# A step count of the dense work ahead of each token-row scatter on POOL

## The chip, the cores and the metric

One Trainium2 chip, of which the kernel uses one core. The metric is the device time of one execution in microseconds, as the median of the runs. The engines are TensorE (PE), VectorE (DVE), ScalarE (ACT), GpSimd (POOL) and SyncE (SP), which here only issues transfers.

## What is computed

A block of attention and a mixture of experts over x of shape (2, 1024, 128), that is 2048 token rows of 128 channels:

```python
x = x + layernorm(attention(layernorm(x)))
x = x + layernorm(ffn(layernorm(x)))

def ffn(x):                              # 64 experts of width 88, 8 of them per token
    scores = sigmoid(x @ gate_w.T)
    choice = scores + gate_bias
    # the best 4 of 8 groups by the sum of their top two, then the best 8 experts in them
    w = scores[chosen] / sum(scores[chosen]) * 2.5
    routed = sum over chosen e of w[e] * (silu(x @ Wg[e].T) * (x @ Wu[e].T)) @ Wd[e].T
    return routed + (silu(x @ Sg.T) * (x @ Su.T)) @ Sd.T
```

## The kernel before

The 2048 tokens are four quads of 512 (16 tiles of 128). After the attention and the routing, the experts are computed in two ways. Quads 2 and 3 (`DENSE`) go through all 64 experts. Quads 0 and 1 (`SPARSE`, eight tiles, `ST = 8`) are sorted by expert: each token row is written eight times, once for each chosen expert, into an array `pair_x` in HBM at a slot that the routing gave; this is the scatter. Later a pair stage, the "burst", reads `pair_x` back in tiles of 128 rows of one expert each, applies that expert and writes `pair_y`, from which eight gathers a tile bring the results back.

**Dense steps.** A step is one of the gate, up and down products of 16 experts' 8 hidden channels for one quad. On TensorE it is six products for gate and up (`gate_up`, L1765 to L1767) and, two steps later (`LAG = 2`), a down product (`down`, L1794, recorded as two matmuls). ScalarE applies SiLU (L1004), VectorE multiplies by the route weight (L1308) and then the two halves (L1318); this last instruction raises the semaphore `s_hid` by one. Steps 0 to 7 are the shared expert (L1507 on VectorE), steps 8 to 15 the first routed ones, and from step 16 on come rounds of eight steps; the burst stands after round 4, so after step 47. When step n has been through VectorE, `s_hid` is n + 1.

**Scatters.** POOL issues 64 scatters (`scatter`, L743): for tile t of the eight and chosen expert k of the eight, an indirect DMA of 128 rows of 512 bytes. `POOL_ORDER` (written out by hand) puts scatters I0 and I1, which are k = 0 to 3 of tile 0, between the last operations of the routing, and I2 to I31 behind all of them. Before the first scatter of a tile POOL waits until all eight of the tile before have landed:

```python
if half == 0:
    pool.wait_ge(s_slots, t + 1)
    if t >= 1:
        pool.wait_ge(s_scat[t - 1], 16 * CHOSEN)
```

Behind the scatters POOL has nothing but the gathers, which wait for the burst's last results (L754).

**What waits for the scatters.** Only SyncE. It issues transfers in a fixed order: dense weights into `w_raw` (`reload`, L630, which waits for the down product that frees the buffer), after each of them three pieces of the weights of the burst (`gu_w`, `down_w`, L614), and, ahead of the dense weights number 27:

```python
if n == BEFORE - 1:
    load_late(len(late))
    for t in range(ST):
        sp.wait_ge(s_scat[t], 16 * CHOSEN)
    for g in range(4):
        load_pairs(g)
```

`load_pairs` (L620) reads four tiles of `pair_x`. Just ahead of it stands `reload(26)`, which waits for the down product of step 45. On TensorE the burst begins with `turn_pairs` (L1945), which waits for the first of these loads.

Of the kernel before, what the change touches and what calls it, by code (L numbers as in the profile page):

```python
# [54 lines left out]
def build(nc, x, w_basis_t, w_v, b_v, w_o_t, b_o, gate_w_t, gate_bias, w_experts, w_shared_up,  # L55
# [21 lines left out]
    CHOSEN = TOP_GROUPS * GE // 4  # L77
# [17 lines left out]
    with ExitStack() as ctx:  # L95
# [8 lines left out]
        def sem(name):  # L104
            return ctx.enter_context(nc.semaphore(name))
# [194 lines left out]
        s_hid = sem("hidden_ready")  # L300
# [151 lines left out]
        SHARED_STEPS = QUADS * SHARED  # L452
# [96 lines left out]
        SUM_AT = {at + 2: t for at, t in WEIGH_AT.items()}  # L549
        MOMENTS_AT = {at + 3: t for at, t in WEIGH_AT.items()}  # L550
        FINISH_AT = {at + 5: t for at, t in WEIGH_AT.items()}

        block = ctx.enter_context(nc.Block())

# [115 lines left out]
        def _(pool):  # L670
# [61 lines left out]
            def scatter(n):  # L732

                t, half = n // 4, n % 4
                if n == 0:
                    pool.wait_ge(s_fill, 16 * (PAIR_TILES // 8))
                    pool.wait_ge(s_xn2, len(SPARSE))
                if half == 0:
                    pool.wait_ge(s_slots, t + 1)
                    if t >= 1:  # L740
                        pool.wait_ge(s_scat[t - 1], 16 * CHOSEN)
                for k in (2 * half, 2 * half + 1):
                    g.indirect_dma_start(  # L743
                        pair_x, bass.IndirectOffsetOnAxis(ap=slots[:, t, k:k + 1], axis=0),
                        x2_rows[:, t, :], None).then_inc(s_scat[t], 16)
# [110 lines left out]
            for what, q, _ in POOL_ORDER:  # L856
                if what in "SX":
                    inv_sqrt(NORMS.index((what, q)), buffer_of(what, q), what == "X")
                elif what == "D":
                    inv_sqrt_att(q)  # L860
                elif what == "B":
                    make_select()
                elif what == "K":
                    make_rank_constants()
                elif what == "I":
                    scatter(q)
                elif what == "P":
                    norm_x(q)
                elif what == "M":
                    write_route(q)  # L870
                elif what == "F":
                    add_bias(q)
                elif what == "J":
                    mask_groups(q)
                elif what == "L":

                    pool.wait_ge(s_shhi, q + 1)
                    n = WD if q == 0 else GATE_AT + REST
                    g.tensor_tensor(sh_lo[:, q, 0:n], sh_raw[:, q, 0:n], sh_hi[:, q, 0:n],
                                    ALU.subtract).then_inc(s_shlo, 1)  # L880
                elif what == "R":
                    split_lo(q)
                elif what == "E":
                    low_part(q)
# [269 lines left out]
        def _(dve):  # L1154
# [275 lines left out]
            def moments(t):  # L1430

                own = t % 2
                if t == 0:
                    dve.wait_ge(s_ysht, len(SPARSE))
                dve.wait_ge(s_red, t + 1)
                link(tt(total[:, own, :], total[:, own, :], shared_y[:, t, :], ALU.add))
                link(v.bn_stats(f_stats[:, own, :], total[:, own, :]))
                v.bn_aggr(f_mv[:, own, :], f_stats[:, own, :]).then_inc(s_fvar, 1)

            def finish(t):  # L1440

                own = t % 2
                dve.wait_ge(s_frstd, t + 1)
                link(v.tensor_scalar(total[:, own, :], total[:, own, :], f_mv[:, own, 0:1],
                                     f_rstd[:, own:own + 1], ALU.subtract, ALU.mult))
                tt(x_sb[:, t, :], total[:, own, :], x1_sb[:, t, :], ALU.add).then_inc(s_fy, 1)
# [69 lines left out]
            for r, k in ROUND_STEPS:  # L1516
# [12 lines left out]
                if at in MOMENTS_AT:  # L1529
                    moments(MOMENTS_AT[at])  # L1530
                if at in FINISH_AT:
                    finish(FINISH_AT[at])

# [581 lines left out]
```

## Time and profile before

| | us |
|---|---|
| median of 3 runs | 421.49 |
| lowest and highest | 420.11 and 421.81 |
| span of the profiled execution | 451.5 |
| mean granted clock of TensorE in it | 0.952 |

The span runs from the first to the last instruction of the one execution that was profiled; a separate time of that execution is not given. It is 30.0 us longer than the median of the timed runs, so a sum of microseconds read from the profile has to say whether the stretch it stands on is there in the timed runs too. Times in the profile are counted from the span's start. The stages are, roughly: attention and routing to 100 us, with the first dense steps from some 75 us on; dense steps with the scatters beside them from 86 to 200 us; the burst to 304 us; dense steps with the gathers beside them, and the sparse tiles' last norms, to the end.

### The profile page before, as it was taken

What the parts mean: (1) busy time and instruction counts of PE and PEld (TensorE: products, weight loads), DVE (VectorE), ACT (ScalarE), POOL (GpSimd) and SP (SyncE); (2) the same over time, 40 slices, a digit from 0 to 9 for tenths busy, and PEclk for the clock granted to TensorE, in tenths of its full rate; (3) what the DMA queues carried; (4) which work ended last, traced back from release to release, by engine and by line L of the source; (5) the groups of instructions that cost most, each with busy time, mean ns of one, the idle gap of its engine ahead of it and who ended that gap; (6) DMA issues with size and microseconds to landing.
All of it is one profiled execution on the core that took longest, in us unless ns stands there. A gap on an engine that the chain in (4) does not pass through costs nothing.

```text
span 451.5 us, 7319 instructions
## 1 busy us (share of the span) xinstructions
PE 399.2 (88%) x2023; PEld 301.9 (67%) x2024; DVE 288.2 (64%) x761; ACT 212.9 (47%) x557; POOL 184.8 (41%) x242
## 2 busy tenths in 40 slices
PE   7889997789999969979999999999749979897784
PEld 5779775355665646646999999996526656564563
DVE  5756987854566635661666666546338867694884
ACT  3668884234234312322666666663144524453424
POOL 7574554666665456600000000004734747667001
PEclk9999996789999998996999999999969989999998
DMA  6369200011489866223666666542211313231001
GB/s 174 112 247 404 97 2 1 12 37 46 159 260 298 203 165 162 81 78 110 179 181 171 181 180 174 168 116 76 71 47 54 99 46 99 82 94 54 13 6 46
DMA packets 65467, 54.03 MB, mean 120 GB/s; under 512 B 7013, under 2 KB 61333, under 8 KB 65429
## 3 DMA queue, kind: packets, MB, share of 16 engines
q1 hardware_dynamic: 60469, 44.85, 33.3%
q0 software_dynamic: 4096, 8.40, 6.4%
q10 hardware_dynamic: 864, 0.33, 0.3%
q8 instruction: 18, 0.29, 0.3%
q14 instruction: 20, 0.16, 0.1%
HBM read 31.53 MB, written 22.02 MB: 119 GB/s over the span
## 4 chain that ended last, share of the span: by engine, by line
PE 67%; DVE 11%; another core or an unknown queue 7%; issue 5%; POOL 5%; ACT 3%; DMA 1%; POOLq 0%; DVEq 0%; SPq 0%; ACTq 0%
PE ps L1794 13%; PE ps L1967 9%; PE ps L1765 8%; PE ps L1767 8%; PE ps L1766 8%; PE ps L1992 6%; PE ps L1945 3%; PE ps L1979 3%; DVE up_w L1308 3%; DVE hid L1318 2%; PE ps L1717 2%; PE ps L1656 1%; PE ps L1705 1%; PE ps L1898 1%
## 5 line engine op out<-in xcount | busy, mean ns | idle before, releaser
L1765 PE MATMUL ps<-x_hi,w_hi 128*128 128x512 f32 (+1 forms) x184 | 98.3, 534 | 25.9 <-DVE hid L1318 24.4
L754 POOL DMA_INDIRECT picked<-pair_y,slots x64 | 62.9, 983 | 137.2 <-DMA pair_y<-pair_out 118.7
L1004 ACT ACTIVATE ps<-ps 128x512 f32<-128x512 f32 (+1 forms) x92 | 51.6, 564 | 137.0 <-PE ps L1767 78.5
L1308 DVE TENSOR_TENSOR up_w<-ps,route_w 128x512 f32<-128x512 f32 (+1 forms) x92 | 61.2, 665 | 73.4 <-remote 31.4
L1794 PE MATMUL ps<-hid,w_raw 128*128 128x512 f32 (+1 forms) x182 | 94.1, 600 | 0.6 <-DVE hid L1318 0.6
L743 POOL DMA_INDIRECT pair_x<-x_rows,slots x64 | 62.5, 977 | 39.5 <-issue 21.0
L1765 PEld LDWEIGHTS ps<-x_hi,w_hi 128*128 128x128 f32 x184 | 35.5, 193 | 62.8 <-issue 34.8
L1767 PE MATMUL ps<-x_hi,w_lo 128*128 128x512 f32 (+1 forms) x184 | 72.3, 393 | 0.0
L1766 PE MATMUL ps<-x_lo,w_hi 128*128 128x512 f32 (+1 forms) x184 | 71.9, 391 | 0.0
L1318 DVE TENSOR_TENSOR hid<-ps,up_w 128x512 f32<-128x512 f32 (+1 forms) x92 | 61.5, 668 | 6.0 <-issue 2.3
L1401 DVE COPY pair_ht<-ps 88x256 f32<-88x256 f32 x64 | 26.9, 421 | 37.4 <-PE ps L1979 30.8
L1967 PE MATMUL ps<-gu_w,pair_xt 128*128 x256 | 50.0, 318 | 0.0
L1766 PEld LDWEIGHTS ps<-x_lo,w_hi 128*128 128x128 f32 x184 | 35.4, 192 | 17.8 <-issue 13.5
L1794 PEld LDWEIGHTS ps<-hid,w_raw 128*128 128x128 f32 x182 | 35.3, 198 | 8.8 <-issue 1.0
L1767 PEld LDWEIGHTS ps<-x_hi,w_lo 128*128 128x128 f32 x184 | 35.4, 192 | 7.6
L1967 PEld LDWEIGHTS ps<-gu_w,pair_xt 128*128 128x128 f32 x256 | 38.9, 192 | 1.4 <-issue 1.0
L1992 PE MATMUL ps<-down_w,pair_ht 88*128 x256 | 39.2, 275 | 0.1
L1035 ACT COPY pair_out<-ps 128x256 f32<-128x256 f32 x64 | 23.9, 373 | 22.8 <-PE ps L1992 22.8
L1992 PEld LDWEIGHTS ps<-down_w,pair_ht 88*128 88x128 f32 x256 | 33.6, 191 | 0.3 <-issue 0.3
L1945 PE MATMUL ps<-ident,pair_in 128*128 128x128 f32 x128 | 25.3, 279 | 4.1 <-DMA pair_in<-pair_x 3.7
L1028 ACT ACTIVATE pair_g<-ps 128x176 f32<-128x176 f32 x64 | 20.3, 318 | 16.0 <-PE ps L1967 15.9
L1019 ACT COPY pair_xt<-ps 128x256 f32<-128x256 f32 x64 | 24.1, 377 | 6.2 <-PE ps L1945 6.2
(220 smaller groups left out, 586.1 us busy)
## 6 DMA issues: line engine op xcount, KB each, us to landing
w_raw<-in_w_experts SPq DMA_DIRECT2D x44, 192.0 KB
pair_x<-zero SPq DMA_DIRECT2D x16, 512.0 KB, 5.6
pair_in<-pair_x SPq DMA_DIRECT2D x32, 256.0 KB, 3.0
pair_y<-pair_out SPq DMA_DIRECT2D x64, 128.0 KB, 2.2
gu_w<-in_w_experts SPq DMA_DIRECT2D x22, 256.0 KB
down_w<-in_w_experts SPq DMA_DIRECT2D x16, 176.0 KB
pair_x<-x_rows,slots POOLq DMA_INDIRECT x64
picked<-pair_y,slots POOLq DMA_INDIRECT x64
```

Of the source, the lines that this page charges most:

```text
L743: g.indirect_dma_start(pair_x, bass.IndirectOffsetOnAxis(ap=slots[:, t, k:k + 1], axis=0), x2_rows[:, t, :], None).then_inc(s_scat[t], 16)
L754: g.indirect_dma_start(picked[:, t % 3, k, :], None, pair_y, bass.IndirectOffsetOnAxis(ap=slots[:, t, k:k + 1], axis=0)).then_inc(s_pick[t ...
L1004: a.activation(bank, bank, ACT.Silu).then_inc(s_gated, 1)
L1308: v.tensor_tensor(up_w[:, k % 2, 0:w], ps[:, gate_bank(k) + 1, 0:w], route_w[:, group, 512 * dense_at(q) + lo:512 * dense_at(q) + lo + w], ...
L1318: v.tensor_tensor(hid[:, s % DEEP, 0:w], ps[:, gate_bank(k), 0:w], up_w[:, k % 2, 0:w], ALU.mult).then_inc(s_hid, 1)
L1765: t_.matmul(out_, hi, mhi, start=start, stop=False)
L1766: t_.matmul(out_, hi, mlo, start=False, stop=False)
L1767: return t_.matmul(out_, lo, mhi, start=False, stop=stop)
L1794: t_.matmul(ps[:, acc_bank(q) if lo == 0 else 6, 0:w], weights_[0:n, WD:WD + P], hid[0:n, s % DEEP, 0:w], start=start, stop=stop).then_inc ...
L1945: mm = t_.transpose(ps[:, 4, P * t:P * t + P], pair_in[:, g % 4, 2 * (u % 2) + t, :], ident[:])
L1967: mm = t_.matmul(ps[:, 2 + u % 2, 256 * t:256 * t + 2 * HID], pair_xt[:, u % 2, P * t:P * t + P], own[:, :, :, 0:PACK], start=True, stop=True)
L1992: mm = t_.matmul(ps[:, pair_bank(u), P * t:P * t + P], pair_ht[:, u % 2, P * t:P * t + P], rows[:, bass.ds(at[t], C)], start=True, stop=True)
```

## The change

From the second tile on, each scatter also waits for `s_hid`. `SHARED_STEPS` is 8 and `CHOSEN` is 8:

```diff
         FINISH_AT = {at + 5: t for at, t in WEIGH_AT.items()}
+        STEPS_A_TILE = 5
...
                 for k in (2 * half, 2 * half + 1):
+                    if t >= 1:
+                        pool.wait_ge(s_hid, SHARED_STEPS + 1 + (STEPS_A_TILE * (CHOSEN * (t - 1) + k)) // CHOSEN)
                     g.indirect_dma_start(
                         pair_x, bass.IndirectOffsetOnAxis(ap=slots[:, t, k:k + 1], axis=0),
                         x2_rows[:, t, :], None).then_inc(s_scat[t], 16)
```

For tile 1 the counts are 9, 9, 10, 10, 11, 12, 12, 13 for k = 0 to 7; for tile 2 they begin at 14, for tile 3 at 19, and so on by five; the last scatter, tile 7 and k = 7, waits for 43. The order of the instructions on each engine is the same in both kernels; the 56 scatters carry one more wait each. The wait for the landing of the tile before stays.

## Rows read from the trace of the kernel before

**Rows 1.** The page: span, busy time by engine, and the shares of the chain by engine.

```profile
span 451.5 us, 7319 instructions
...
PE 399.2 (88%) x2023; PEld 301.9 (67%) x2024; DVE 288.2 (64%) x761; ACT 212.9 (47%) x557; POOL 184.8 (41%) x242
...
PE 67%; DVE 11%; another core or an unknown queue 7%; issue 5%; POOL 5%; ACT 3%; DMA 1%; POOLq 0%; DVEq 0%; SPq 0%; ACTq 0%
```

**Rows 2.** Timeline of TensorE, 161 to 175 us, the down products of the dense steps.

```profile
161.60 1.02 PE L1794 MATMUL ps<-hid,w_raw 128*128 128x512 f32 x2
...
163.85 1.02 PE L1794 MATMUL ps<-hid,w_raw 128*128 128x512 f32 x2
...
171.08 1.79 PE L1794 MATMUL ps<-hid,w_raw 128*128 128x512 f32 x2
...
174.09 1.02 PE L1794 MATMUL ps<-hid,w_raw 128*128 128x512 f32 x2
```

**Rows 3.** The chain of waits, pieces of unknown release in order of time: start, us, what.

```profile
160.32 6.92 another core or an unknown queue
...
324.49 9.76 another core or an unknown queue
```

**Rows 4.** Timeline of SyncE's queue, 174 to 203 us.

```profile
177.46 23.14 SPq L630 DMA_DIRECT2D w_raw<-in_w_experts  x6
200.89 2.03 SPq L620 DMA_DIRECT2D pair_in<-pair_x  x4
```

**Rows 5.** The chain of waits, 200 to 205 us: what stands before the pair stage.

```profile
200.27 0.33 SPq L630
200.89 2.81 DMA pair_in<-pair_x
203.84 0.68 PE ps L1945 x2
```

**Rows 6.** Timeline of POOL, first and last scatters of tiles 1 to 3.

```profile
101.62 0.96 POOL L743 DMA_INDIRECT pair_x<-x_rows,slots  x1 [2.02 <-DMA pair_x<-x_rows,slots]
...
107.94 0.96 POOL L743 DMA_INDIRECT pair_x<-x_rows,slots  x1 [0.30 <-issue]
...
110.47 0.96 POOL L743 DMA_INDIRECT pair_x<-x_rows,slots  x1 [0.30 <-issue]
113.44 0.96 POOL L743 DMA_INDIRECT pair_x<-x_rows,slots  x1 [2.01 <-issue]
...
126.59 0.96 POOL L743 DMA_INDIRECT pair_x<-x_rows,slots  x1 [3.31 <-DMA pair_x<-x_rows,slots]
```

**Rows 7.** Timeline of POOL, first scatters of tiles 4 to 7, the last of tile 5 and the last of all.

```profile
140.21 0.96 POOL L743 DMA_INDIRECT pair_x<-x_rows,slots  x1 [3.60 <-DMA pair_x<-x_rows,slots]
...
154.62 1.13 POOL L743 DMA_INDIRECT pair_x<-x_rows,slots  x1 [4.54 <-DMA pair_x<-x_rows,slots]
...
163.64 0.96 POOL L743 DMA_INDIRECT pair_x<-x_rows,slots  x1 [0.30 <-issue]
168.71 1.13 POOL L743 DMA_INDIRECT pair_x<-x_rows,slots  x1 [4.11 <-DMA pair_x<-x_rows,slots]
...
180.89 0.96 POOL L743 DMA_INDIRECT pair_x<-x_rows,slots  x1 [2.19 <-issue]
...
189.74 0.96 POOL L743 DMA_INDIRECT pair_x<-x_rows,slots  x1 [0.30 <-issue]
```

**Rows 8.** Timeline of VectorE, the step counter's 9th and 11th to 13th increments.

```profile
101.03 0.69 DVE L1318 TENSOR_TENSOR hid<-ps,up_w 128x512 f32<-128x512 f32 x1
...
106.34 0.69 DVE L1318 TENSOR_TENSOR hid<-ps,up_w 128x512 f32<-128x512 f32 x1
...
111.74 0.69 DVE L1318 TENSOR_TENSOR hid<-ps,up_w 128x512 f32<-128x512 f32 x1
...
113.12 0.69 DVE L1318 TENSOR_TENSOR hid<-ps,up_w 128x512 f32<-128x512 f32 x1
```

**Rows 9.** Timeline of POOL in the gathers: one that has a wait already fulfilled.

```profile
353.08 0.95 POOL L754 DMA_INDIRECT picked<-pair_y,slots  x1 [0.30 <-issue]
```

## The prediction

> **What bounds the kernel now.** I read the page first. TensorE is busy 88% of the span and holds 67% of the chain that ended last, while POOL is busy 41% and holds 5% of it [rows 1]. So POOL's scatters cost time only where something on TensorE's way waits for them. About half a per cent, 2.1 us, is what a measurement of this kernel can tell from no change.
>
> Next I read the dense steps beside the scatters, on TensorE's timeline. The down products of successive steps start 2.25 us apart (161.60, 163.85): six gate and up products and a down product with nothing between them. One gap stands out: from 163.85 the next down product starts at 171.08, 7.23 us on, and the one after it 3.01 us later [rows 2]. Against 2.25 us a step this loses 4.98 + 0.76 = 5.7 us. The chain puts its cause, 6.92 us from 160.32 on, on a release that the profile does not name; the largest piece of that kind is 9.76 us at 324.49 [rows 3], and in all they are 7% of the chain [rows 1], about 31 us. The profiled span of 451.5 us exceeds the median of 421.5 us by 30.0 us, nearly the same amount. I therefore take these gaps as belonging to the profiled execution and not to the timed runs, and place the timed runs on the trace by taking 5.7 us out of all times behind 171 us.
>
> Then the place where the scatters are waited for. SyncE issues six dense weights between 177.46 and 200.6 us, each when a dense step frees its buffer, and the pair loads at 200.89 [rows 4]. In the chain the pair stage on TensorE stands behind the load (200.89, 2.81 us), and this behind a dense weight's issue, not behind a scatter [rows 5]. With 5.7 us taken out, the timed runs' **deadline** for the last landing is 200.9 - 5.7 = 195.2 us.
>
> Last, when the scatters come in. On POOL one scatter starts 1.265 us after another (107.94 to 110.47 is two of them): 0.96 of work and 0.30 between. At each new tile POOL stands until the tile before has landed: 2.02, 2.01, 3.31 us [rows 6], then 3.60, 4.54, 4.11 and 2.19 us; the last of all starts at 189.74 [rows 7]. From tile 1's first start at 101.62 to tile 7's at 180.89 that is 13.2 us a tile. The last has been generated at 190.7 and by the light landings (2.0 us) is in at 192.7: 2.5 us ahead of the deadline.
>
> **The change, part by part.**
> The wait itself, where it is already fulfilled. Nothing shows a scatter with such a wait, but a gather has one: the first of tile 3 waits for a sum that was long there, and stands 0.30 us behind its predecessor like the gathers that have no wait [rows 9]. Cost nothing; upper bound 0.02 us, since a larger gap would show in the digits, for 56 scatters about 1 us on POOL alone.
>
> Tile 1. The counter's ninth increment is the instruction at 101.03 (ends 101.72), the eleventh ends at 107.03, the twelfth at 111.74 + 0.69 = 112.43, the thirteenth at 113.81 [rows 8]. The scatter k = 0 waits for 9 and moves by 0.1 us. Those at k = 1 to 4 want 9, 10, 10 and 11 and move by 0.1 us at most. But k = 5 wants 12 and started at 107.94: it now starts at 112.43, **4.5 us** later. It cannot come sooner, since TensorE in that stretch still spreads the routing weights and the dense step is late by itself. The k = 7 wants 13 at 113.81 and by POOL's own pace comes at 114.96: no further wait.
>
> Tiles 2 to 7. Five dense steps are 5 x 2.25 = 11.25 us, while POOL on its own needs 13.2 us a tile, so the counts run away from POOL by 2 us a tile and no later wait holds for long. Tile 2's first wants 14, some 2.3 us behind 13, so 116.1; POOL can only be there at 113.44 + 4.5 = 117.9. Everything behind is the old sequence, 4.5 us later. So the change does not spread the scatters, except in tile 1; it moves them back. The last starts at 189.74 + 4.5 = 194.2, is generated at 195.2 and lands at **197.2 us**.
>
> Who is queued behind and who waits. POOL's queue behind the scatters is the gathers, idle for over 100 us before their turn, so they do not care. On SyncE the pair loads wait, and with them the 27th dense weights, which are needed only behind the burst. SyncE is not held before that. The transfers themselves are the same in number and size; a shift by 4.5 us among late weights costs TensorE nothing, as its steps there wait for no load.
>
> The sum. In the profiled execution 197.2 is still 3.7 us before 200.9: 0. In the timed runs 197.2 - 195.2 = 2.0 us late, if every landing there is as slow as in the trace. One of them is not a fair sample: tile 5's last scatter starts at 163.64 and its landing wait of 4.11 us lies inside the unexplained gap (160.32 to 167.24) that I took out of the steps. Taking the light 2.2 us instead gives back 1.9 us. Left are 0.1 us: 451.5 us would become 451.6 us, and the median 421.5 becomes **421.6 us**. The bounds from the rows: with all landings at 2.0 us the scatters would be ready 7 us before the above, so 0; with all as in the trace and tile 1's landing moved into the busy stretch (3.3 instead of 2.0 us), 3.3 us late.
>
> The other way to cost a landing is a rule. The rows have 2.0 to 4.5 us from the end of a scatter's generation to its landing [rows 6, 7]. The Trainium skill (DMA: Bandwidth & Descriptors, Anatomy of one DMA, the SWDGE path) gives such a transfer a fixed 2.0 us and its bytes at 436 GB/s, so an estimated 2.15 us for 64 KB. The light rows agree, the four of the busy stretch do not. By the rule the last scatter would land near 190 us even with the change, and the time would be 421.5 us; by the rows as they stand it would be 423.5 us.
>
> **The rivals.**
> *Late pairs* (slower). The scatters land as slowly in the timed runs as in the trace, and the burst starts when they do. Place: SyncE's wait ahead of the pair loads. Price: 2.0 to 3.3 us, and up to 1 us for the 56 added waits. It decides from 195.2 us on; it is told from no change when the landing is behind 197.3. For it: the margin before is only 2.5 us against a shift of 4.5. Against it: the busy landings may be as much a product of the profiled execution as the gaps are. Time 421.5 + 3.3 = 424.8 us.
>
> *A gap less* (faster). The unexplained gap beside the scatters is in the timed runs too, in part, and comes from eight scatters generated in one run; the change breaks the run of tile 1 and shifts the rest against the weights' loads. Price: at most 5.7 us, so 415.8 us; half of it gives 418.6 us. For it: the gaps stand only in the two stretches with indirect DMAs. Against it: the 30.0 us, which leave no room for them in the timed runs, and that from tile 2 on the runs of eight stay whole.
>
> *The counts hold everywhere.* If landings and generation are quicker in the timed runs than 11.25 us a tile, each wait holds, the scatters are really spread, and the last starts with count 43, which is step 42 and five steps before step 47: 11 us before the burst. Landed 3 us later it is still ahead of the deadline: 421.5 us. This is no change as well.
>
> **How the numbers follow.** Late by less than 2.1 us or not at all, with the counts holding or not: 0.56, within 0.5%. Late pairs by more: 0.28, slower. A gap less: 0.16, faster. The range takes in late pairs with the waits' cost (425.5) and half the gap (418.6); I put its low end at 418.0.
>
> **What would show it.** In the profile of the changed kernel: the sixth scatter of tile 1 waits some 4.5 us for L1318 on VectorE; from tile 2 on POOL's idle time before a tile's first scatter is still put on landings; the last scatter starts near 194 us; the pair loads are issued where they were, unless the profiled execution has lost its gap at 160 us, and then SyncE waits some us for POOL's scatters. Wrong would be: waits for VectorE before scatters of tiles 3 to 7, a last scatter before 190 us, or a dense step that is not 2.25 us.

## The result, and the profile after

| | median, us | lowest and highest | runs |
|---|---|---|---|
| before | 421.35 | 419.78 and 425.70 | 20 |
| changed | 424.68 | 423.11 and 427.33 | 20 |

The ratio is 1.0093, with a 95% interval from 1.0078 to 1.0108: the change makes the kernel 3.3 us slower by the medians and 3.9 us by the ratio (3.3 to 4.6 by its interval). That is the side of the rival *late pairs* (424.8 us), to which the prediction gave 0.28, not of its forecast of 421.6 us; the range held it. Of the runs below, one execution of the kernel before (501.97 us) and one with the counts two lower (567.12 us) stood at a far lower granted clock; they are in the medians given and not in the ratios.

The page of the changed kernel, against [rows 1]:

```profile
span 424.1 us, 7319 instructions
...
PE 389.6 (92%) x2023; PEld 300.5 (71%) x2024; DVE 288.6 (68%) x761; ACT 213.0 (50%) x557; POOL 184.0 (43%) x242
...
PE 54%; POOL 23%; issue 8%; DVE 7%; ACT 3%; DMA 3%; POOLq 0%; DVEq 0%; SPq 0%; ACTq 0%
POOL picked L757 15%; PE ps L1797 9%; PE ps L1970 9%; PE ps L1995 7%; PE ps L1768 5%; PE ps L1770 5%; PE ps L1769 5%; PE ps L1948 4%; PE ps L1982 3%; PE ps L1720 2%; POOL xn L818 2%; POOL pair_x L746 1%; POOL rstd L787 1%; DVE stats L1175 1%; PE ps L1708 1%
```

The profiled execution took 425.83 us over all, with a span of 424.1, so 1.7 us lie around a span. The chain names no unknown release any more: the gaps of [rows 3] are not in it. Of POOL's 23% the gathers at the end are 15%; these are no work of the change, since a profile of the kernel before without the gaps, shown below, has them too (POOL 22%, gathers 15%). What that profile does not have is the scatters in the chain (L746, 1%, which is 4 us).

POOL's timeline, scatters of tile 1 (105.05 to 115.27), the first of tiles 2 to 7, and the last of all (against [rows 6] and [rows 7]):

```profile
105.05 0.96 POOL L746 DMA_INDIRECT pair_x<-x_rows,slots  x1 [4.37 <-DVE hid L1321]
...
110.09 0.96 POOL L746 DMA_INDIRECT pair_x<-x_rows,slots  x1 [0.30 <-issue]
115.27 0.96 POOL L746 DMA_INDIRECT pair_x<-x_rows,slots  x1 [4.22 <-DVE hid L1321]
...
120.75 0.96 POOL L746 DMA_INDIRECT pair_x<-x_rows,slots  x1 [2.00 <-DMA pair_x<-x_rows,slots]
...
134.04 0.96 POOL L746 DMA_INDIRECT pair_x<-x_rows,slots  x1 [3.46 <-DMA pair_x<-x_rows,slots]
...
148.15 0.95 POOL L746 DMA_INDIRECT pair_x<-x_rows,slots  x1 [4.30 <-issue]
...
161.85 0.96 POOL L746 DMA_INDIRECT pair_x<-x_rows,slots  x1 [3.91 <-issue]
...
176.59 0.96 POOL L746 DMA_INDIRECT pair_x<-x_rows,slots  x1 [4.83 <-issue]
...
188.93 0.95 POOL L746 DMA_INDIRECT pair_x<-x_rows,slots  x1 [2.46 <-issue]
...
197.77 0.96 POOL L746 DMA_INDIRECT pair_x<-x_rows,slots  x1 [0.30 <-issue]
```

VectorE's timeline, the step counter's ninth, eleventh and twelfth increments (against [rows 8]):

```profile
103.58 0.69 DVE L1321 TENSOR_TENSOR hid<-ps,up_w 128x512 f32<-128x512 f32 x1
...
108.91 0.69 DVE L1321 TENSOR_TENSOR hid<-ps,up_w 128x512 f32<-128x512 f32 x1
...
114.30 0.69 DVE L1321 TENSOR_TENSOR hid<-ps,up_w 128x512 f32<-128x512 f32 x1
```

Tile 1's first scatter waits for count 9 (103.58 + 0.69 = 104.27) and its sixth for count 12 (114.30 + 0.69 = 114.99). From tile 2 on POOL stands for landings again, 2.0 to 4.8 us each, and the counts are passed without a wait (the view names the landing for tiles 2 and 3 and no releaser for the later ones; no scatter behind tile 1 stands for VectorE longer than the usual 0.3 us). The last scatter starts at 197.77.

SyncE's queue at the turn from the dense weights to the pair loads, and the chain of waits there (start, us, what), against [rows 4] and [rows 5]:

```profile
174.55 20.90 SPq L631 DMA_DIRECT2D w_raw<-in_w_experts  x6
200.12 2.03 SPq L621 DMA_DIRECT2D pair_in<-pair_x  x4
```

```profile
197.77 2.27 DMA pair_x<-x_rows,slots
200.12 2.88 DMA pair_in<-pair_x
203.14 0.67 PE ps L1948 x2
```

The sixth dense weight is issued by 174.55 + 20.90 = 195.45 us. The pair loads would follow 0.3 us later, but come at 200.12, right behind the last landing (197.77 + 2.27 = 200.04). The chain before the pair stage now runs through scatters, where in [rows 5] it ran through a dense weight. TensorE waits 8.1 us for the first pair load.

### The profile page after: what moved, and what is told of

Its sections match the earlier page's. It is cut to its first block, busy times and chain, and to the rows that moved or that the text cites. A ratio compares the mean times of both kernels' runs of the same rounds, so it can differ in the third digit from the quotient of the medians.

```text
span 424.1 us, 7319 instructions
## 1 busy us (share of the span) xinstructions
PE 389.6 (92%) x2023; PEld 300.5 (71%) x2024; DVE 288.6 (68%) x761; ACT 213.0 (50%) x557; POOL 184.0 (43%) x242
## 4 chain that ended last, share of the span: by engine, by line
PE 54%; POOL 23%; issue 8%; DVE 7%; ACT 3%; DMA 3%; POOLq 0%; DVEq 0%; SPq 0%; ACTq 0%
POOL picked L757 15%; PE ps L1797 9%; PE ps L1970 9%; PE ps L1995 7%; PE ps L1768 5%; PE ps L1770 5%; PE ps L1769 5%; PE ps L1948 4%; PE ps L1982 3%; PE ps L1720 2%; POOL xn L818 2%; POOL pair_x L746 1%; POOL rstd L787 1%; DVE stats L1175 1%; PE ps L1708 1%
## 5 line engine op out<-in xcount | busy, mean ns | idle before, releaser
L1768 PE MATMUL ps<-x_hi,w_hi 128*128 128x512 f32 (+1 forms) x184 | 102.1, 555 | 2.4 <-DVE hid L1321 1.3
L1797 PE MATMUL ps<-hid,w_raw 128*128 128x512 f32 (+1 forms) x182 | 91.5, 586 | 0.6 <-DVE hid L1321 0.6
L746 POOL DMA_INDIRECT pair_x<-x_rows,slots x64 | 62.0, 968 | 47.0 <-issue 28.9
L1770 PE MATMUL ps<-x_hi,w_lo 128*128 128x512 f32 (+1 forms) x184 | 71.1, 386 | 0.0
L1769 PE MATMUL ps<-x_lo,w_hi 128*128 128x512 f32 (+1 forms) x184 | 70.6, 384 | 0.0
L1321 DVE TENSOR_TENSOR hid<-ps,up_w 128x512 f32<-128x512 f32 (+1 forms) x92 | 61.5, 668 | 7.6 <-ACT ps L1007 3.5
L1797 PEld LDWEIGHTS ps<-hid,w_raw 128*128 128x128 f32 x182 | 34.2, 192 | 8.3 <-issue 1.0
L1396 DVE TENSOR_TENSOR pair_h<-ps,pair_g 128x176 f32<-128x176 f32 x64 | 20.9, 327 | 13.3 <-ACT pair_g L1031 13.3
```

The costliest lines, as they stand in the source:

```text
L746: g.indirect_dma_start(pair_x, bass.IndirectOffsetOnAxis(ap=slots[:, t, k:k + 1], axis=0), x2_rows[:, t, :], None).then_inc(s_scat[t], 16)
L1321: v.tensor_tensor(hid[:, s % DEEP, 0:w], ps[:, gate_bank(k), 0:w], up_w[:, k % 2, 0:w], ALU.mult).then_inc(s_hid, 1)
L1768: t_.matmul(out_, hi, mhi, start=start, stop=False)
L1769: t_.matmul(out_, hi, mlo, start=False, stop=False)
L1770: return t_.matmul(out_, lo, mhi, start=False, stop=stop)
L1797: t_.matmul(ps[:, acc_bank(q) if lo == 0 else 6, 0:w], weights_[0:n, WD:WD + P], hid[0:n, s % DEEP, 0:w], start=start, stop=stop).then_inc ...
```

## The experiments

Every kernel was timed against the kernel before in the same session; ratios are to that, with 95% intervals. Its median was 421.26, 420.24, 420.94 and 421.05 us in the four sessions; a ratio can differ by up to 0.3% from the quotient of the two medians. Two theories stand against each other. **L**: the only cost is that the last scatter lands after SyncE's turn for the pair loads, and TensorE starts the pair stage later by that much. **C**: the counts cost by themselves, as 56 waits, or by where they put the scatters against the other transfers.

### The kernel before, profiled again

> The kernel before once more, for a profile without the unexplained gaps. Theory L (the scatters land later than SyncE's turn for the pair loads): 421.4 us, span near 419.5; the last scatter of POOL starts near 191.5 us and the pair loads are issued near 195.5 us, behind a dense weight and not behind a scatter; TensorE waits some 3.5 us for them. Rival C (the shifted scatters cost time by contention or by the waits themselves): the pair loads stand where they stand in the changed kernel, near 200 us, and the gap of 3.3 us lies elsewhere.

Measured: 419.97 us (before 421.26; ratio 0.9985, 0.9953 to 1.0018), span 417.6. POOL's timeline, the first scatters of tiles 1, 2, 6 and 7, and the last of all; SyncE's queue; TensorE at the start of the pair stage:

```profile
100.84 0.96 POOL L743 DMA_INDIRECT pair_x<-x_rows,slots  x1 [2.03 <-DMA pair_x<-x_rows,slots]
...
112.65 0.96 POOL L743 DMA_INDIRECT pair_x<-x_rows,slots  x1 [2.01 <-DMA pair_x<-x_rows,slots]
...
167.15 0.96 POOL L743 DMA_INDIRECT pair_x<-x_rows,slots  x1 [4.36 <-DMA pair_x<-x_rows,slots]
...
178.97 1.12 POOL L743 DMA_INDIRECT pair_x<-x_rows,slots  x1 [2.02 <-DMA pair_x<-x_rows,slots]
...
187.97 1.08 POOL L743 DMA_INDIRECT pair_x<-x_rows,slots  x1 [0.30 <-issue]
```

```profile
172.11 20.07 SPq L630 DMA_DIRECT2D w_raw<-in_w_experts  x6
192.47 2.02 SPq L620 DMA_DIRECT2D pair_in<-pair_x  x4
```

```profile
195.72 0.66 PE L1945 MATMUL ps<-ident,pair_in 128*128 128x128 f32 x2 [3.96 <-DMA pair_in<-pair_x]
...
197.33 3.62 PE L1794 MATMUL ps<-hid,w_raw 128*128 128x512 f32 x4
```

The page's chain, by engine:

```profile
PE 54%; POOL 22%; DVE 9%; issue 8%; DMA 3%; ACT 3%; POOLq 0%; SPq 0%; DVEq 0%; ACTq 0%
```

Without the gaps the last scatter starts at 187.97 us. SyncE's turn is at 172.11 + 20.07 = 192.18, the pair loads start at 192.47, and TensorE waits 3.96 us for them. How soon could they start by the scatters alone? In the profiles where they stand right behind the last landing, they start 2.35 us behind the start of the last scatter (200.12 less 197.77 with the change; the same in six runs below, and 2.7 and 2.8 us in two). By that they could start at 190.3. So the kernel before has about 2 us in hand: near the 2.5 us that the prediction read first, and not the 4.4 us that it reckoned with in the end.

### The waits themselves

```diff
-                        pool.wait_ge(s_hid, SHARED_STEPS + 1 + (STEPS_A_TILE * (CHOSEN * (t - 1) + k)) // CHOSEN)
+                        pool.wait_ge(s_hid, 1)
```

> The 56 added waits are kept, but each asks for a count of 1, which is long reached. L: the waits cost nothing by themselves, 421.4 us. Rival C, the waits' own cost: 56 times 0.03 to 0.08 us on POOL, the scatters 2 to 4 us later, 422 to 424.7 us.

Measured: 421.13 us, ratio 1.001 (0.9985 to 1.0036), and 0.30 us between two scatters as before. A wait on a count long reached costs nothing that can be measured, which removes the first form of C; the interval ends at 0.36%, well below the loss. One thing in this profile is not in the expectation: no scatter is held, and yet the landing waits are longer than in the kernel before (5.76 us ahead of tile 6), the last scatter starts at 191.04 in place of 187.97 us, and the pair loads come 0.6 us late. Whether that is the execution or the 56 waits is open; the run from tile 5 on, below, shows the same.

### The counts for tile 1 alone

```diff
-                    if t >= 1:
+                    if t == 1:
                         pool.wait_ge(s_hid, SHARED_STEPS + 1 + (STEPS_A_TILE * (CHOSEN * (t - 1) + k)) // CHOSEN)
```

> The counts are kept for tile 1 alone (8 waits of 56). L: all of the shift comes from there, 424.7 us as with the whole change. Rival (each of the 56 waits adds its part): about an eighth of the loss, below 422 us.

Measured: 424.50 us, ratio 1.0102 (1.0061 to 1.0143), the whole loss with eight of 56 waits. POOL (tile 1's first and sixth scatter, tile 2's first, the last of all), SyncE, the last landing in the chain of waits, and TensorE:

```profile
101.78 0.95 POOL L746 DMA_INDIRECT pair_x<-x_rows,slots  x1 [2.95 <-DVE hid L1321]
...
111.98 0.96 POOL L746 DMA_INDIRECT pair_x<-x_rows,slots  x1 [4.19 <-DVE hid L1321]
...
117.47 0.96 POOL L746 DMA_INDIRECT pair_x<-x_rows,slots  x1 [2.01 <-DMA pair_x<-x_rows,slots]
...
194.38 0.96 POOL L746 DMA_INDIRECT pair_x<-x_rows,slots  x1 [0.30 <-issue]
```

```profile
171.17 21.00 SPq L631 DMA_DIRECT2D w_raw<-in_w_experts  x6
196.72 2.03 SPq L621 DMA_DIRECT2D pair_in<-pair_x  x4
```

```profile
194.38 2.26 DMA pair_x<-x_rows,slots
```

```profile
199.69 0.66 PE L1948 MATMUL ps<-ident,pair_in 128*128 128x128 f32 x2 [7.94 <-DMA pair_in<-pair_x]
```

This profile and that of the kernel before are in step up to the pair stage: the last dense step's instruction on VectorE (L1318 there, L1321 here) starts at 191.67 and at 191.66. So they can be laid on each other. Tile 1's first scatter comes 0.9 us later, tile 2's 4.8 us later (117.47 against 112.65), and the last of all 6.4 us later (194.38 against 187.97), since the landings of tiles 2, 5 and 6 took 0.5 to 0.8 us more each. The pair loads come 4.25 us later (196.72 against 192.47): 6.4 us less the 2 us in hand. TensorE waits 7.9 in place of 4.0 us, and the span is 3.8 us longer (421.4 against 417.6). What the pair loads are late is nearly what the span is longer. And since the dense steps end at the same time in both, the shifted scatters cost them nothing.

### The counts from tile 2 on

```diff
-                    if t >= 1:
+                    if t >= 2:
                         pool.wait_ge(s_hid, SHARED_STEPS + 1 + (STEPS_A_TILE * (CHOSEN * (t - 1) + k)) // CHOSEN)
```

> The counts are kept from tile 2 on, tile 1 is free. L, worked out with the counter's times of the changed kernel: tile 2's first scatter would be ready at 114.5 us and waits for 14 at 118.6, its last for 18 at 129.3, so tile 2 ends some 0.4 us ahead of where it ends with the whole change: 424.3 us. My statement on record, that only tile 1 is held, taken to the letter: 421.4 us.

Measured: 423.21 us, ratio 1.0043 (1.0015 to 1.0071). The first scatters of tiles 1 and 2 on POOL's timeline, and tile 2's last:

```profile
102.22 0.96 POOL L746 DMA_INDIRECT pair_x<-x_rows,slots  x1 [2.02 <-DMA pair_x<-x_rows,slots]
...
117.44 0.96 POOL L746 DMA_INDIRECT pair_x<-x_rows,slots  x1 [5.42 <-DVE hid L1321]
...
127.60 0.95 POOL L746 DMA_INDIRECT pair_x<-x_rows,slots  x1 [1.50 <-DVE hid L1321]
```

POOL stands 5.42 us ahead of the first scatter of tile 2, for its count of 14, where a landing alone takes 2.0, and 1.50 us ahead of the last, where 0.30 is the usual. The pair loads come 2.4 us behind the end of the dense weights' issue, against 4.7 with the whole change. So tile 2's counts would hold too if tile 1's had not moved it already; the loss is somewhat smaller than expected, as the lateness is.

### The counts from tile 5 on

```diff
-                    if t >= 1:
+                    if t >= 5:
                         pool.wait_ge(s_hid, SHARED_STEPS + 1 + (STEPS_A_TILE * (CHOSEN * (t - 1) + k)) // CHOSEN)
```

> The counts are kept from tile 5 on (24 waits). By the counter of the runs so far tile 5 wants 29, reached near 150 us, and is ready for its first scatter at 153 us, so no count is ever waited for. Theory L (only a late last landing costs): 421.3 us. Rival (the counts cost by where the scatters meet the late weights, or per wait): above 422 us.

Measured: 419.77 us, ratio 0.998 (0.9949 to 1.0011): no cost, as L has it. No count holds: tile 5's, the 29th, is there at 149.6 us, ahead of the end of the scatter before (149.8), although the view puts the 4.36 us of the landing wait behind it on VectorE. As in the run with fulfilled waits the late landings are long (4.90 us ahead of tile 6), the last scatter starts at 190.43, and the pair loads are 0.5 us later than SyncE's turn allows, too little to be seen in the time.

### All counts two lower, and two higher

```diff
-                        pool.wait_ge(s_hid, SHARED_STEPS + 1 + (STEPS_A_TILE * (CHOSEN * (t - 1) + k)) // CHOSEN)
+                        pool.wait_ge(s_hid, SHARED_STEPS - 1 + (STEPS_A_TILE * (CHOSEN * (t - 1) + k)) // CHOSEN)
```

> All 56 counts two lower. Tile 1's sixth scatter then wants 10, reached at 103.7 us, ahead of POOL; tile 2's first wants 12 at 111.7 us, POOL is there at 112.6 us; no count holds. L: 421.3 us. Rival: as the whole change, 424.7 us.

Measured: 422.60 us, ratio 1.0037 (1.0017 to 1.0058). I expected no loss. In its profile tile 2's first scatter still waits for VectorE (3.31 us in place of 2.0), as the dense steps are 3 us later in this execution than in the one that the expectation was worked out from. The landings behind it are long (up to 5.57 us), so the pair loads are 1.8 us behind the dense weights' end. The two together use up the 2 us in hand.

The other direction has `SHARED_STEPS + 3`:

> All 56 counts two higher. Tile 1's sixth scatter wants 14, 3.6 us behind 12, and all behind it moves by as much; the pair loads come 3.6 us later than with the change, each microsecond one of the time: 428.3 us. Rival (the loss is not the lateness but something that the shift of tile 1 does once): 425 us.

Measured: 427.52 us, ratio 1.0149 (1.0133 to 1.0166). SyncE's queue:

```profile
175.29 20.47 SPq L631 DMA_DIRECT2D w_raw<-in_w_experts  x6
204.81 1.48 SPq L621 DMA_DIRECT2D pair_in<-pair_x  x3
```

The pair loads come 9.05 us behind the dense weights (175.29 + 20.47 = 195.76), and TensorE waits 12.2 us for them. The loss grows with the lateness: 6.3 us by the ratio. The 9 us are from the one profiled execution, the slowest of the four, which took 430.06 us, 9.1 us above the median before.

### Two tiles in flight, without and with the counts

```diff
-                    if t >= 1:
-                        pool.wait_ge(s_scat[t - 1], 16 * CHOSEN)
+                    if t >= 2:
+                        pool.wait_ge(s_scat[t - 2], 16 * CHOSEN)
```

> The kernel before, but a tile's first scatter waits for the landing of the tile before the last, not of the last. L: POOL needs 10.1 us a tile in place of 13.2, the last landing comes some 15 us sooner, near 176 us, and the pair loads stand at 192.4 us behind a dense weight: 420.5 to 421.3 us, since before lies within 1 us of its deadline.

> The whole change, but with the wait for the landing moved to the tile before the last. L: POOL is now quicker than the counts, so each scatter really follows its count; the last wants 43, reached near 181 us, and lands near 185 us, 7 us ahead of SyncE's turn: 421 us, the loss is gone although all 56 counts are there. Rival (the counts themselves cost, by pacing): 424 us or more.

Measured: 420.15 us without the counts, ratio 0.9975 (0.9946 to 1.0004), and 419.96 us with all 56 of them, ratio 0.9976 (0.9945 to 1.0008). POOL's timeline of the second (tile 2's first, tile 7's first, the last of all), and SyncE's queue:

```profile
115.94 0.96 POOL L746 DMA_INDIRECT pair_x<-x_rows,slots  x1 [0.62 <-issue]
...
172.80 0.96 POOL L746 DMA_INDIRECT pair_x<-x_rows,slots  x1 [1.28 <-DVE hid L1321]
...
181.66 0.96 POOL L746 DMA_INDIRECT pair_x<-x_rows,slots  x1 [0.30 <-issue]
```

```profile
171.41 20.58 SPq L631 DMA_DIRECT2D w_raw<-in_w_experts  x6
192.29 2.03 SPq L621 DMA_DIRECT2D pair_in<-pair_x  x4
```

Here POOL is quicker than the counts and follows them to the end: tile 7's first waits for VectorE. The last scatter starts at 181.66, and the pair loads stand 0.3 us behind the dense weights (171.41 + 20.58 = 191.99), as in the kernel before. The 56 counts are all there, the scatters are spread as the change was to spread them, and the loss is gone. With the run of tile 1 alone, where the shifted scatters left the dense steps as they were, this removes the second form of C.

### Lateness and loss, all runs

This takes in all runs with the pair loads in their old place in SyncE's order. Lateness is the start of the pair loads less the end of the sixth dense weight's issue, from each run's one profile; where nothing is late it is 0.3 us. The loss is the ratio less one.

| kernel | lateness, us | loss |
|---|---|---|
| before, again | 0.29 | -0.15% |
| before, two in flight | 0.29 | -0.25% |
| counts, two in flight | 0.30 | -0.24% |
| counts from tile 5 | 0.81 | -0.20% |
| waits long fulfilled | 0.88 | +0.10% |
| counts less 2 | 1.79 | +0.37% |
| counts from tile 2 | 2.39 | +0.43% |
| counts for tile 1 | 4.55 | +1.02% |
| the change | 4.67 | +0.93% |
| counts plus 2 | 9.05 | +1.49% |

No run whose interval shows a loss is on time, and none that is on time or less than 1 us late has one. Each lateness is that of one execution, each loss that of several. Together with the pair of the change and the same counts with two tiles in flight, this shows L.

### A version that beats both

If the deadline is SyncE's turn, it can be moved. With two tiles in flight the scatters are in long before, so the first four pair loads can be issued two dense weights sooner:

```diff
-                if n == BEFORE - 1:
+                if n == BEFORE - 3:
                     load_late(len(late))
...
-                    if t >= 1:
-                        pool.wait_ge(s_scat[t - 1], 16 * CHOSEN)
+                    if t >= 2:
+                        pool.wait_ge(s_scat[t - 2], 16 * CHOSEN)
```

> As the kernel before with two tiles in flight, and SyncE issues the first four pair loads ahead of the dense weights number 25, not 27, so 4 dense steps (9 us) sooner. If the deadline is SyncE's turn and not the scatters, TensorE's wait of 4.0 us at the start of the pair stage goes, and with it the lower clock behind it: 416 to 417.5 us. If the time is bound elsewhere: 421 us.

Measured: **413.84 us**, ratio 0.9831 (0.9793 to 0.9870), more than expected. SyncE's queue and TensorE's timeline:

```profile
171.81 11.19 SPq L630 DMA_DIRECT2D w_raw<-in_w_experts  x4
183.29 2.06 SPq L620 DMA_DIRECT2D pair_in<-pair_x  x4
```

```profile
191.38 0.38 PE L1945 MATMUL ps<-ident,pair_in 128*128 128x128 f32 x2
...
192.49 1.88 PE L1794 MATMUL ps<-hid,w_raw 128*128 128x512 f32 x4
```

The loads are issued at 183.29, TensorE turns the first pairs at 191.38 with no wait, and the four late down products (L1794) take 1.88 us where they took 3.62 in the kernel before. The stages 190 to 200 and 200 to 210 us show why (busy us of each engine with counts, then the granted clock, DMA share and GB/s); first the kernel before, then this version:

```profile
190.00:200.00 10.00, 5.58 (x14) 2.65 (x14) 1.84 (x4) 1.63 (x4) 0.00 (x0) 0.78 0.43 125
200.00:210.00 10.00, 10.00 (x66) 8.92 (x65) 4.28 (x12) 5.01 (x16) 0.00 (x0) 0.88 0.39 111
```

```profile
190.00:200.00 10.00, 9.54 (x54) 7.05 (x54) 4.06 (x10) 4.66 (x14) 0.00 (x0) 1.00 0.28 79
200.00:210.00 10.00, 10.00 (x83) 9.82 (x82) 6.26 (x17) 6.43 (x21) 0.00 (x0) 1.00 0.57 164
```

In the kernel before, where TensorE is idle for 4 us, it was granted 0.78 and 0.88 of its full clock in these stretches, so part of each at 1.2 and part at 2.4 GHz. Without the idle time it keeps 1.00. What that is worth can be read off: the pair stage starts 4.3 us sooner (191.38 for 195.72), its third transposes already 7.1 us sooner (194.81 for 201.92), and the span is 6.9 us shorter. So some 2.8 us were lost behind the wait, in the first 6 us of the stage, where the clock is the lower one for a part. I had counted the wait and too little for the clock.

The early pair loads alone, with the landing wait of the kernel before:

> The kernel before, landing waits untouched, with only the first four pair loads moved ahead of the dense weights number 25. Theory L: SyncE is there at 183 us but the last scatter lands at 191.1 us, so the pair loads come at 191.2 in place of 192.5 us: 1.2 us gained, 419.5 us. Rival (the order on SyncE alone gives the gain of the last version): 414 us.

Measured: 418.98 us, ratio 0.9963 (0.9930 to 0.9995), in line with some 1.2 us gained and far from 414. SyncE's queue:

```profile
174.52 12.26 SPq L630 DMA_DIRECT2D w_raw<-in_w_experts  x4
192.19 2.03 SPq L620 DMA_DIRECT2D pair_in<-pair_x  x4
```

SyncE is done with the four dense weights at 186.78, and the pair loads stand 2.35 us behind the start of the last scatter (189.84): now the last landing sets them. This one profiled execution was the fastest of twelve (415.83 us), with the dense steps 3.6 us later than in the kernel before profiled again (last instruction on VectorE at 195.23 for 191.67) and the scatters only 1.9 us, so TensorE did not wait for the loads at all. In such an execution the early loads alone give the whole gain; at the median they don't. And the counts on top of the best version:

> The version with two tiles in flight and early pair loads, and the whole change's 56 counts on top. The last scatter starts at 181.7 us as in the run with counts and two in flight, lands near 185 us, so the pair loads come at 185 in place of 183.3 us, still 7 us ahead of TensorE's need: 414 us, as without the counts. Rival (counts cost in themselves): 416 us or more.

Measured: 413.24 us, ratio 0.983 (0.9796 to 0.9865), the same as without them. So both parts are needed to have the gain in every execution, and the counts are neutral there too.

## Why the prediction was wrong in its likeliest case

- **What bounds.** Right: TensorE's dense steps, 2.24 us each, with the pair stage behind SyncE's pair loads, and the scatters of cost only through them.
- **The gaps.** Right that they belong to that one profiled execution: in none of the thirteen profiles taken since, of the changed kernel and of twelve experiments, does the chain put anything on an unknown release.
- **The shift.** Forecast 4.5 us, all from the sixth scatter of tile 1. Measured 4.8 at tile 2 (117.47 less 112.65 in two profiles in step): 0.9 from the first scatter's count, forecast at 0.1, and the rest from the sixth. It varies: in the profile of the changed kernel POOL stands 4.37 us ahead of the first scatter, as in that execution the dense steps were 3.3 us later and the scatters only 1.9 (ninth increment 103.58 for 100.29, tile 0's last scatter 99.72 for 97.85). "Everything behind is the old sequence, 4.5 us later" did not hold: at the last scatter the shift is 6.4 us. That these landings are longer because of the shift is not shown; they are as long in the two runs in which no count holds.
- **Tiles 2 to 7 unaffected.** Right as things are, since POOL is slower (13.0 us a tile) than the counts (11.2). Taken alone their counts do hold, as the run from tile 2 on shows.
- **The waits cost nothing fulfilled.** Right: ratio 1.001.
- **The margin: the step that failed.** The prediction set 192.7 us for the last landing and 195.2 for the deadline, 2.5 us apart, and then gave back another 1.9 us by replacing tile 5's landing wait of 4.11 us with 2.2, since it lay inside a gap: 4.4 us in hand against a shift of 4.5, so 0.1 us. The kernel before without gaps has about 2 us in hand (2.15: 192.47 less 187.97 + 2.35). Its tile 5 landing takes 4.36 us (the idle time ahead of 167.15), with no gap near, so the 1.9 us were not there to give back. With the measured terms the sum is 6.4 - 2.15 = 4.25 us of lateness in place of 0.1: 1.9 from the give-back, 1.9 from the shift, 0.35 from the first reading of the margin. It became 3.8 us of span, and 3.3 to 3.9 us at the medians.
- **The place of the timed runs on the trace.** Taking 5.7 us out of the steps was not enough: the last dense step stands at 191.67 instead of 200.08, which is 8.4 us. The last scatter, of which nothing was taken, stands 1.8 us sooner (187.97 for 189.74). That the last scatter of the run of tile 1 alone starts at 194.38, beside a forecast of 194.2, is luck: 1.8 us sooner before and 1.9 us more of shift.
- **Why landings are long.** In the clean profile POOL's waits for them are 2.0 us while the core's DMA engines are busy 0.10 of the time, and 3.1 to 4.4 us while they are busy 0.50 to 0.94 of it, with the burst's weights under way. These weights are the likely cause; no run took them away, so it is not shown.
- **The landing time by a rule.** The estimate of 2.15 us by the Trainium skill (DMA: Bandwidth & Descriptors, Anatomy of one DMA) is for a whole transfer, its setup included. The last landing in the chain agrees, 2.26 us from the start of the scatter's generation; the four among the late weights do not (POOL waits 3.1 to 4.4 us in the clean profile, behind 0.96 of generation). The measured rows decide: by the figure of the Trainium skill no loss would have come.
- **The rivals.** *Late pairs* was the case that came, at its price (424.8 against 424.7), though the price was made up of other terms. *A gap less* had nothing to stand on. *The counts hold everywhere* is what two tiles in flight make true, and it costs nothing, as worked out.
- **Two rough sums.** Late pairs with 1 us for the waits would be 425.8 us, not 425.5, and landings at 2.0 us all through would save 7.8 us, not 7. The forecast does not rest on either.

The margin was read from a profile whose execution was 30 us off the timed ones, and the one row in it that spoke for a loss was explained away. The upper bound of the sum (3.3 us) was near the time that came, though it had one landing longer, by 1.3 us, where three were, by 1.9 in all, and a deadline 2.7 us too late; the choice between the bounds was not.

## What to carry to other kernels

A wait added "beside" other work costs what it takes from the slack of the last thing behind it; look for the one place where the chain of transfers meets the busy engine, and measure the slack there in a profile whose span agrees with the timed runs. If a producer needs 13 us for what the pace allows 11, a pace can only delay it. When a whole stage waits at its entry for a load, first ask whether the load's turn in its queue can come sooner: here that was worth 1.7%, nearly twice what the pacing lost.

## What the runs showed of the hardware that was not expected

- One profiled execution can carry some 31 us that no timed run has, in pieces of up to 9.8 us put on an unknown queue, all of them in stretches with indirect DMAs. What causes them stays open; no run was made for it.
- An idle time of 4 us on TensorE was followed by a stretch with part of it at the lower clock (0.78 and 0.88 granted), which cost some 2.8 us more at the start of a stage: removing the wait shortened the span by 6.9 us, and the time by 6.4 us by the medians and 7.1 by the ratio.
- A landing is seen sooner by SyncE than POOL's idle time suggests: the chain has the last scatter in at 2.26 us from the start of its generation (in five profiles; 2.6 and 2.7 in two), while POOL's next scatter starts 2.96 us from there (0.96 of generation and 2.0 idle, of which 0.3 stand between any two scatters). A margin read off POOL's waits comes out too small by up to 0.7 us.
- The profiled executions differ by up to 5 us at the 100 us mark: the ninth increment of the counter starts at 100.1 to 101.7 us in the eight where the first 20 us were granted a clock of 1.00, and at 101.7 to 105.3 us in the six where it was 0.91. The scatters do not move by as much (in two of the six 1.9 and 2.1 us where the dense steps moved by 3.3 and 3.6), so this alone moves the two against each other by some 1.4 us. A margin of 2 us is therefore more in some executions and less in others.
